# Query bias added by VectorE at the evacuation, causal mask on 64 rows, second norm of batch 0 at the later batches' slots

## What is computed

```
xn  = layernorm(x)
out = x + attention(xn) + ffn(xn)
# attention: q = (layernorm(xn)*g + b) @ Wq ; k, v = split(xn @ Wkv); 16 heads of 64
#   q, k l2-normalised and scaled, 2 null keys/values per head in front
#   sim = 8*q.k - slope[h]*|i-j| ; causal ; softmax ; @ v ; @ Wout
# ffn: 8 tokens over 16 experts give a capacity of 8 // 16 = 0 rows per expert,
#   so nothing is added and it is layernorm(xn)*ln_g + ln_b
```

## Time and profile before

| | |
|---|---|
| median of 3 runs | 2932.53 us (2931.27 to 2934.16) |
| profiled execution, its own time | 2933.4 us |
| its span in the trace | 2931.5 us |
| PE busy | 2748.9 us (94%) |
| DVE busy | 2428.2 us (83%) |
| ACT busy | 2194.7 us (75%) |
| POOL busy | 2172.8 us (74%) |

### The profile page before, as it was taken

How to read it: one execution, slowest core, us unless ns; L and a number is a source line. 1 busy time by engine, 2 the same in 40 slices (tenths; PEclk the granted TensorE clock), 3 DMA queues, 4 the chain that set the end, 5 groups by cost and what they waited for, 6 DMA issues and landing times.

```text
span 2931.5 us, 83165 instructions
## 1 busy us (share of the span) xinstructions
PE 2748.9 (94%) x31119; PEld 1579.5 (54%) x31119; DVE 2428.2 (83%) x6258; ACT 2194.7 (75%) x3380; POOL 2172.8 (74%) x2458
## 2 busy tenths in 40 slices
PE   3589999999999999999999999999999999999997
PEld 3245555555555555555555555555555555555554
DVE  6778888888888888888888888888888888888786
ACT  3577787777777777777777777777777777877775
POOL 6786677966788677885879767796678867788663
PEclk7799999999999999999999999999999999999999
DMA  4122343322443335423444234333243333542222
GB/s 153 45 49 55 67 86 84 86 61 65 92 93 69 65 66 91 100 57 68 74 87 97 59 66 83 83 89 62 63 96 88 70 66 68 89 98 54 46 50 62
DMA packets 629566, 220.07 MB, mean 75 GB/s; under 512 B 593584, under 2 KB 595632, under 8 KB 629168
## 3 DMA queue, kind: packets, MB, share of 16 engines
q1 hardware_dynamic: 627696, 214.67, 34.7%
q10 hardware_dynamic: 1472, 0.09, 0.0%
HBM read 55.23 MB, written 16.78 MB: 25 GB/s over the span
## 4 chain that ended last, share of the span: by engine, by line
PE 65%; POOL 16%; DVE 8%; issue 4%; DMA 3%; ACT 3%; SPq 1%; POOLq 0%; ACTq 0%; DVEq 0%
PE PS L1232 10%; PE PS L1207 8%; PE PS L1211 8%; PE PS L1210 8%; PE PS L1255 4%; PE PS L1280 4%; PE PS L1282 3%; POOL RN L785 3%; PE PS L1284 3%; PE PS L1301 3%; PE PS L1236 3%; PE PS L1302 3%; PE PS L1303 3%; PE PS L1263 2%; POOL AR L774 2%
## 5 line engine op out<-in xcount | busy, mean ns | idle before, releaser
L1018 DVE CUSTOM_DVE_ANT_0 PS<-PS,STR 128x512 f32<-128x512 f32 (+3 forms) x1536 | 821.4, 579 | 160.9 <-PE PS L1255 160.0
L570 ACT ACTIVATE AR<-PS,SC 128x1024 f32<-128x1024 f32 (+1 forms) x640 | 657.0, 1027 | 213.9 <-PE PS L1263 94.1
L1207 PE MATMUL PS<-WH,XT 128*128 128x388 f16 x2048 | 677.9, 331 | 46.3 <-DVE AR L1025 35.0
L785 POOL TENSOR_TENSOR RN<-SS,HALF 128x8 f32<-128x8 f32 x256 | 488.4, 1908 | 288.6 <-DVE SS L1097 283.5
L1210 PE MATMUL PS<-WL,XT 128*128 128x388 f16 x2048 | 677.8, 331 | 0.0
L1211 PE MATMUL PS<-WH,XT 128*128 128x388 f16 x2048 | 677.6, 331 | 0.0
L574 ACT ACTIVATE AR<-AR 128x1024 f16<-128x1024 f32 (+1 forms) x640 | 621.8, 972 | 20.3
L1053 DVE TENSOR_TENSOR AR<-AR 128x768 f16<-128x768 f32 (+1 forms) x448 | 510.4, 1155 | 18.7 <-ACT AR L574 18.7
L1232 PE MATMUL PS<-AR 64*128 64x512 f16 (+3 forms) x4608 | 498.2, 325 | 5.4 <-ACT AR L570 5.3
L1280 PE MATMUL PS<-AR 128*128 128x66 f16 x4608 | 475.5, 193 | 20.9 <-POOL AR L774 11.9
L1282 PE MATMUL PS<-AR 128*128 128x64 f16 x4608 | 473.9, 194 | 0.0
(11 more groups left out here) (234 smaller groups left out, 5358.6 us busy)
## 6 DMA issues: line engine op xcount, KB each, us to landing
XW<-in_L_attn_x SPq DMA_DIRECT2D x112, 256.0 KB, 2.9
out<-ACC SPq DMA_DIRECT2D x64, 256.0 KB, 2.3
ACC<-in_L_attn_x SPq DMA_DIRECT2D x56, 256.0 KB, 2.9
AR<-QKB SPq DMA_TRANSPOSE x512, 2.5
AR<-in_L_attn_Wkv SPq DMA_DIRECT2D x2, 1536.0 KB, 13.9
ACC<-in_L_attn_x SPq DMA_DIRECT2D x2, 1024.0 KB, 7.5
AR<-in_L_attn_Wout SPq DMA_DIRECT2D x1, 2048.0 KB, 9.7
AR<-CTK SPq DMA_TRANSPOSE x128, 2.4
```

The lines of the kernel that those rows point to most:

```text
L570: e.activation(PR[:, n % 2, :, 0:wide], SB[:, :, 0:wide], ACT.Exp, scale=SIG).then_inc(s_p, 1)
L785: e.tensor_tensor(RN[:, i % 2, :], SS[:, i % 2, :], HALF[:, :], ALU.pow).then_inc(s_rn, 1)
L1018: e.tensor_tensor_reduce(out=r[:, 0:n], in0=r[:, 0:n], in1=ST[:, u % 2, h, o:o + n], scale=1.0, scalar=LOW, op0=ALU.add, op1=ALU.max, accu ...
L1207: e.matmul(PJ, XT[:, k, xs], WH[:, k, p, :], start=k == 0, stop=False)
```

## The change

1. **Bias.** L1209 goes, and `ONB`, `BQR`, and GpSimd's splitting with them. The bias stays in fp32 in `BQF` (128 x 8 x 132, the same row in all partitions; ScalarE scales it once before `s_ready`). ScalarE's copy takes only the 128 key columns; a new VectorE instruction adds 132 columns of `PJ` and `BQF` into `QKB`, behind ScalarE's value copy and ahead of the old L1025. `QKB`'s buffer waits (`s_kq`, `s_nsc`) now also stand on VectorE; the projection waits for the new semaphore `s_qb`, and so does the square.
2. **Mask.** `TRI` is 128 x 2 x 128: rows 0 to 63 and rows 64 to 127 hold the same two masks, one for each half of a 128-token block. Per block and head two matmuls of 64 rows and 64 columns take the place of one of 128 rows and 128 columns: 2048 of them for 1024. GpSimd builds `TRI` with six instructions for two.
3. **Second norm.** `due_base` goes; batch 0 goes by the tables of the later batches.
4. **Tables.** All slot tables but the lists of late weights have new numbers, and `HOLD` too.

```diff
-W_PROJ = [z for z in [1, 7, 15, 25, 29, 33, 40, 42] for k in range(KC)]
+W_PROJ = [z for z in [6, 11, 16, 20, 31, 36, 42, 44] for k in range(KC)]
...
-W_BN = [81, 88, 103, 110, 121, 135, 149, 184]
+W_BN = [83, 89, 98, 111, 124, 138, 153, 184]
...
-def due_base(slot, when, first):
-
-    out = [(0, t) for t in range(NT) if SL + 6 * t + first == slot]
-    return out + [(b, t) for b, t in due(slot, when, NB, BL) if b]
...
+            w.wait_ge(s_scd, 1)
+            w.wait_ge(s_bqe, 3)
+            e.activation(BQF[:, :, :], BQF[:, :, :], ACT.Copy, scale=SC[:, 14:15]).then_inc(s_bqf, 1)
...
-                    e.activation(QKB[:, g % 3, t % 2, 0:260], PJ[:, 0:260], ACT.Copy).then_inc(s_kvev, 1)
+                    e.activation(QKB[:, g % 3, t % 2, 0:128], PJ[:, 0:128], ACT.Copy).then_inc(s_kvev, 1)
...
+                    w.wait_ge(s_qb, 2 * i + 2)
...
-                for b, t in due_base(s, W_BN, 4):
+                for b, t in due(s, W_BN, NB, BL):
...
-            pc(e.memset(TRI[:, :], 0.0))
-            e.affine_select(out=TRI[:, :], in_=TRI[:, :], compare_op=ALU.is_ge, fill=NEG, base=0,
+            pc(e.memset(TRI[:, :, :], 0.0))
+            for a in range(2):
+                pc(e.affine_select(out=TRI[:, a, :], in_=TRI[:, a, :], compare_op=ALU.is_ge, fill=NEG, base=64 * a - 64,
+                                   pattern=[[-1, P]], channel_multiplier=1))
+            pc(e.memset(TRI[0:64, :, :], 0.0))
+            pc(e.affine_select(out=TRI[0:64, 0, :], in_=TRI[0:64, 0, :], compare_op=ALU.is_ge, fill=NEG, base=0,
+                               pattern=[[-1, P]], channel_multiplier=1))
+            e.affine_select(out=TRI[0:64, 1, :], in_=TRI[0:64, 1, :], compare_op=ALU.is_ge, fill=NEG, base=64,
                             pattern=[[-1, P]], channel_multiplier=1).then_inc(s_tri, 1)
...
-                bq(e.tensor_scalar(raw, raw, SC[:, 14:15], None, ALU.mult))
-                bq(e.tensor_copy(row, raw))
...
+                    w.wait_ge(s_bqf, 1)
                     w.wait_ge(s_vsc, 4 * (b + 1))
+                    if g > 2:
+                        w.wait_ge(s_kq[(g - 3) % 4], 32 * ((g - 3) // 4 + 1))
+                        w.wait_ge(s_nsc, g - 2)
+                    e.tensor_tensor(QKB[:, g % 3, t % 2, 128:260], PJ[:, 128:260], BQF[:, u % NP, :], ALU.add).then_inc(s_qb, 1)
...
-            w.wait_ge(s_bqr, 2)
...
+                        w.wait_ge(s_qb, i)
...
-                if k == 0:
-                    e.matmul(PJ[:, 128:260], ONB[:, :], BQR[:, p, :], start=False, stop=False, skip_group_check=True)
...
-                        for h in range(2):
-                            for kt, off in blocks:
-                                ins = e.matmul(SB[:, h, off:off + P], TRI[:, :], IDB[:, :], start=False, stop=True,
-                                               skip_group_check=True)
-                            ins.then_inc(s_st, 1)
+                        for kt, off in blocks:
+                            for a in range(2):
+                                for h in range(2):
+                                    hs = slice(64 * h, 64 * h + 64)
+                                    to = slice(off + 64 * a, off + 64 * a + 64)
+                                    ins = e.matmul(SB[:, h, to], TRI[hs, a, :], IDB[hs, hs], start=False, stop=True,
+                                                   skip_group_check=True)
+                                    if a and kt == blocks[-1][0]:
+                                        ins.then_inc(s_st, 1)
```

More of the change, by code:

```diff
@@ L62 @@
[L62 to L87, removed]
-W_BN = [81, 88, 103, 110, 121, 135, 149, 184]
-W_BM = [86, 92, 109, 110, 121, 135, 153, 186]
-W_BA = [91, 98, 109, 114, 133, 141, 158, 186]
-HOLD = [6.1, 7.1, 7.8]
+W_PIECE = [48, 53, 55, 61, 65, 66, 67, 80, 82, 86, 88, 91]
+W_MAX = [50, 51, 55, 59, 64, 64, 65, 72, 76, 76, 83, 94]
@@ new lines @@
+W_SCORE = [92, 98, 104, 109, 111, 114, 116, 129, 133, 137]
+W_PLOW = [95, 104, 104, 108, 113, 115, 121, 128, 137, 140]
+W_VALUE = [105, 109, 109, 114, 121, 132, 134, 140, 143, 143]
+W_ON = [108, 146]
+W_OTS = [111, 150]
+W_OTL = [109, 146]
+W_OTT = [115, 156]
+W_OP = [117, 121, 138, 150, 159, 160, 164, 174]
+W_ADD = [115, 118, 138, 147, 157, 159, 161, 166]
+W_PROJ = [z for z in [6, 11, 16, 20, 31, 36, 42, 44] for k in range(KC)]
+W_KV = [3, 10, 16, 24, 33, 37, 42, 46]
+W_VL = [6, 10, 16, 20, 25, 29, 43, 49]
@@ new lines @@
+W_STRIP = [33, 43]
+W_SQ = [14, 24, 43, 48]
+W_SS = [13, 21, 45, 51]
+W_POW = [23, 31, 45, 50]
+W_TP = [38, 46, 60, 68]
+W_HI = [29, 39, 55, 67]
+W_LO = [25, 40, 55, 65]
+W_ROWS = [66, 91]
+W_SHIFT = [69, 96]
+W_CTP = [82, 106]
+W_NX = [78, 107]
+W_NL = [75, 114]
+W_NTT = [93, 136]
+W_XA = [-344, -260, -212, -159, -147, -116, -88, -85]
+W_STAT = [-222, -182, -172, -126, -124, -112, -94, -88]
+W_XB = [-78, -48, -35, -11, 1, 8, 15, 15]
+W_XF = [-54, -45, -32, -10, 2, 3, 16, 20]
+W_XH = [-47, -39, -16, -7, 1, 6, 20, 27]
@@ L95 @@
+W_XL = [-36, -35, -21, -13, 4, 15, 26, 28]
+W_XTP = [-34, -26, -16, 9, 16, 19, 22, 43]
+W_SMALL = [-92, -78, -77, -67, -59]
+W_VSC = [-7]
+W_BASE = [72, 89, 101, 107, 111, 124, 154, 178]
+W_BN = [83, 89, 98, 111, 124, 138, 153, 184]
+W_BM = [83, 84, 96, 112, 121, 134, 152, 182]
+W_BA = [83, 91, 102, 113, 128, 140, 157, 183]
+HOLD = [6.4, 6.7, 6.8]
 LATE_ACT = [0, 1, 5, 6, 9, 10, 15, 16, 18, 24, 25, 27, 32, 33, 38, 39]
@@ L182, in fused_block @@
         ST = STF[:, :].bitcast(BF16).rearrange("p (s h n) -> p s h n", s=2, h=2)
-        BQR = sb("BQR", [P, NP, 132], BF16)
+        BQF = sb("BQF", [P, NP, 132], F32)
         LG = sb("LG", [P, DIM], F32)
@@ L199, in fused_block @@
         IDB = sb("IDB", [P, P], BF16)
-        TRI = sb("TRI", [P, P], BF16)
-        ONB = sb("ONB", [P, P], BF16)
+        TRI = sb("TRI", [P, 2, P], BF16)
         CB = sb("CB", [P, 4, H], F32)
@@ L296, in fused_block @@
         s_wq0, s_wq1, s_wq2, s_wk0, s_wk1, s_wv0, s_wv1 = (mk("s_" + z) for z in ("wq0", "wq1", "wq2", "wk0", "wk1", "wv0", "wv1"))
-        s_pc, s_dc, s_sc, s_msk, s_bqp, s_slp, s_ala = (mk("s_" + z) for z in ("pc", "dc", "sc", "msk", "bqp", "slp", "ala"))
+        s_pc, s_dc, s_sc, s_msk, s_bqf, s_slp, s_ala = (mk("s_" + z) for z in ("pc", "dc", "sc", "msk", "bqf", "slp", "ala"))
         s_id, s_io, s_sig, s_slv, s_ald = (mk("s_" + z) for z in ("id", "io", "sig", "slv", "ald"))
@@ L301, in fused_block @@
         s_am, s_amt, s_dg, s_amb, s_wact, s_spl, s_tri = (mk("s_" + z) for z in ("am", "amt", "dg", "amb", "wact", "spl", "tri"))
-        s_bqr, s_al, s_vsa, s_vn, s_scd, s_won, s_woh = (
-            mk("s_" + z) for z in ("bqr", "al", "vsa", "vn", "scd", "won", "woh"))
+        s_al, s_vsa, s_vn, s_scd, s_won, s_woh = (
+            mk("s_" + z) for z in ("al", "vsa", "vn", "scd", "won", "woh"))
         s_ready, s_ds = mk("s_ready"), mk("s_ds")
@@ L310, in fused_block @@
         s_ct = [mk("s_ct0"), mk("s_ct1")]
-        s_proj, s_kvev, s_vl, s_sq, s_ss, s_rn = (mk("s_" + z) for z in ("proj", "kvev", "vl", "sq", "ss", "rn"))
+        s_proj, s_kvev, s_qb, s_vl, s_sq, s_ss, s_rn = (mk("s_" + z) for z in ("proj", "kvev", "qb", "vl", "sq", "ss", "rn"))
         s_nsc, s_t1, s_hi, s_lo = (mk("s_" + z) for z in ("nsc", "t1", "hi", "lo"))
@@ L740, in _ @@
                 ln_lo(0, t)
-            bq = chain(e, s_bqp)
-            w.wait_ge(s_bqe, 3)
             w.wait_ge(s_scd, 1)
[L745 to L752, removed]
-                bq(e.tensor_scalar(raw, raw, SC[:, 14:15], None, ALU.mult))
-                bq(e.tensor_copy(row, raw))
[L755 to L763, removed]
+            pc(e.tensor_scalar(SC[:, 15:16], SC[:, 14:15], 1e-12 / KA, None, ALU.mult))
+            pc(e.tensor_tensor(SC[:, 15:16], SC[:, 15:16], SC[:, 15:16], ALU.mult))
+            for b in range(2):
+                pc(e.tensor_scalar(CL[:, b, :, 2:4], IDF[:, 0:16].rearrange("p (t c) -> p t c", c=2), 0.0, SC[:, 15:16],
+                                   ALU.mult, ALU.add))
+            ln_vsc(0)
             w.wait_ge(s_ready, 1)
@@ L833, in _ @@
                         ln_vsc(b)
-                for b, t in due_base(s, W_BM, 6):
+                for b, t in due(s, W_BM, NB, BL):
                     i = NT * b + t
@@ L839, in _ @@
                     w.wait_ge(s_base, 3 * i + 1)
-                for b, t in due_base(s, W_BA, 8):
+                for b, t in due(s, W_BA, NB, BL):
                     i = NT * b + t
```

27 lines of the change are left out of this document (4 added, 23 removed).

## The result

The changed kernel takes 2802.16 us (median of 4 runs, 2800.58 to 2806.08); the kernel before took 2933.35 us beside it. The ratio is 0.955, 95% interval 0.954 to 0.956: 131 us or 4.5% faster, where 2.3% was forecast.

The account below looks back on a forecast made before the run. The prediction took PE's work to bound the even part (97% busy): 2933.4 - 29 (bias) - 28 (mask) - 25 (forms) + 20 (addition) - 5 (start and filling) = 2866.4, forecast 2866 us, range 2836 to 2905.

Parts of the forecast that it names:

- PE's work: On TensorE, bias matmul 29 us, mask matmuls 28 us and changes of form 25 us go, 82 us in all.
- A pair of mask matmuls: In the mask, two half-size matmuls run side by side in 0.030 us; gain 28 us, bounds -2 and 30.
- The saved changes of form: In PE's order, 1542 changes of form become 1286; 256 at 0.10 us save 25 us, bounds 20 to 28.
- The rival that rested on it: Small mask matmuls are bound by issue, not columns, so the 28 us are not saved: 2894 us; chance 0.12.
- VectorE's addition: 512 bias additions of 0.28 us, 143 us beside PE's work; 0.3 us a unit reach PE, +20 us, bounds 0 to 60.
- the turnaround of the bank: Projection's bank: shorter ScalarE copy, then the addition, +0.18 us until the next projection; costs nothing, up to 5 us in the filling.
- the new tables also remove waits: Rival: PE's 76 idle us in the even part fall by a quarter, addition hides fully: 2827 us, half 2846; chance 0.15.
- the change does nothing, since PE's idle time was the bound: Rival: PE's idle time, not its work, sets the time, so nothing is gained; excluded by 97% busy, chance 0.01.
- The prediction's own sign of being wrong: PE's idle time in the even part under 70 us or over 130 would show the forecast wrong; 80 to 110 right.
- The slower rival: Projection's bank is freed only behind the late addition, PE stands at L1189, 0.38 us per projection: 3041 us; chance 0.04.
- The filling: From 69 to 216 us, moving batch 0's second norm off the chain takes back 5 us of PE idling, bounds 0 and 12.
- the start: Before the first projection: four more instructions building TRI cost +1.2 us; dropping the bias splitting counts -1.5 us.

Follow-up runs that it names:

- e6: The changed kernel with the bias back as a matmul, GpSimd's splitting and the 260-column copy included: ratio 0.9689 to the kernel before.
- e1: The changed kernel with every slot table and HOLD of the kernel before: 2933.8 us, ratio 0.999 to the kernel before.
- e2: The kernel before with all slot tables and HOLD of the changed kernel, nothing else changed: ratio 0.9855 to the kernel before, 43 us faster.
- e7: The changed kernel with batch 0's second norm back at every 6 slots from slot 52 on: ratio 0.9574 to the kernel before.
- e8: The changed kernel with the bias addition done twice on VectorE, output unchanged: ratio 0.9598 to the kernel before.

## Why the prediction was wrong

**PE's work: right.** 82 us were forecast, 86.5 us of busy time are gone. The bias is worth 30.2 us of busy time (e6 against the changed kernel), forecast 29. A pair of mask matmuls takes 0.029 us, forecast 0.030, so 1024 pairs take 30 us instead of 59, 29 gained for 28. The saved changes of form hold at 0.10 us. By the starts of the matmuls that makes 83 us of work. Busy time is a fair measure of it only where PE stands still equally often, since the last matmul before each stop is drawn some 0.17 us past its work (0.33 us long, where the next one follows after 0.16): 224 stops before and 221 in the changed kernel, but 341 in e1, where so only 54.3 us show for 70 us of work. Work is not time, though: of the mask's 66 us in the new order 36 show, and in the old order 14 of 41.

**The rule of a floor for small matmuls: not here.** The Trainium skill's floor of 25 ns from start to start ("TensorE: Matmul & The Clock Gate", "Wait — 56ns, not 53.3ns?") would make four mask matmuls 0.10 us, an estimate by that page; they take 0.058. The pair is what takes 0.029, and its two starts lie 3 to 11 ns apart, so the floor, if it holds, holds for a pair on both halves of the rows and not for each instruction. The rival that rested on it is refuted.

**VectorE's addition: the duration right, its price wrong.** 0.290 us each for 0.28. "I take 0.3 us a unit, +20 us": the double addition costs 14 us, so the price of the work was about right; but the move as a whole is worth +41 us in the new order, not 29 - 20 = 9. The step counted ScalarE's copy, 0.11 us shorter, for the turnaround of the bank, and not as shortening VectorE's wait behind it. It was said of ScalarE's rest that it "gives nothing"; VectorE's waits for ScalarE (68.4 us in e6, 42.2 in the changed kernel) speak against that, but no run separates it. VectorE is busy 2516.7 us, not some 2570: additions of 0.290 us add only 88.5 us to its busy time, since they overlap their neighbours.

**The step that failed: the tables.** Of the forecast's miss of 64 us, 60 are PE's idle time: the sum had it rise by 15 us (20 for the addition, less 5), and it fell by 45. In the sum the new tables counted only for changes of form; for waits they had no term. They stood in a rival, "the new tables also remove waits", at a chance of 0.15, with 2827 us when its gain and the hiding of the addition are both whole. By e2 they are worth 43 us by themselves. By e1 they are worth 129 us to the other parts, which without them come to nothing. The forecast read "97% busy" as "bound by PE's work". The old order's cap was another: when work was taken from PE in e1, its idle time rose by the same amount. The rival "the change does nothing, since PE's idle time was the bound", excluded by the 97% at a chance of 0.01, is what e1 shows for the parts without the tables. The prediction's own sign of being wrong, idle time in the even part under 70 us, came true: 36.5 us from 216 to 2600. The share of idle time in a stretch says what PE could gain by not waiting; it does not say that PE would not wait more if it had less to do.

**The slower rival: refuted.** The projection's wait for the evacuation is 1.0 us in 1800, for 5.2 before.

**The filling: right in size.** The second norm was forecast at -5 us with bounds 0 and 12; e7 gives 7 to 9 for it. For the start the forecast had -0.3: the first projection starts 1.1 us later, but ScalarE's first copy of it 0.2 us earlier.

## What to carry to other kernels

An engine at 97% is not proof that its work is the bound where several engines walk fixed orders and wait for each other: take some work from it and look whether its idle time grows. When a change comes with a new order, price the order as a part of its own, by running the parts in the old order and the old parts in the new one; the two are not additive (-43 and -3 us alone, -132 together). And don't judge an order by setting one or a few of its tables back: here that cost 18 and 20%.

## What was not expected of the hardware

Two matmuls of 64 rows and 64 columns on the two halves of the array take 0.029 us together: half of what a pair of 128 columns takes (0.055), although each has a weight load of 128 columns that lasts 94 ns in the trace. VectorE could be loaded to 95% of a stretch (e8), and the 144 us of added instructions cost 14 us.
